# Raw-row routers, a split last tile, scatters that are not held and identity matmuls at the seams of a four-stage kernel

## The reference, cut to what matters

```python
x = L0_attn_a_x                                   # [8, 512, 128] float32
x = x + attn_a(layernorm(x))                      # 16 heads of 8, q and k normalized
x = x + ffn(layernorm(x))                         # routed, 8 experts, top 2, capacity 384
x = x + attn_b(layernorm(x))                      # 16 heads of 64, relative position bias
x = x + ffn(layernorm(x))                         # the same experts again

def ffn(x):                                       # N = 4096 tokens
    logits = xf @ w_router                        # [N, 8]
    probs = softmax(logits); gate, eidx = top_k(probs, 2); gate /= sum(gate)
    pos = cumsum(one_hot(eidx)) - 1               # place of each choice in its expert's list
    keep = pos < C                                # C = 384
    expert_in[e, pos] = xf                        # rows to their slots
    h = relu(expert_in @ w1 + b1); out = h @ w2 + b2
    y = sum(out[e, pos] * gate)                   # back to the tokens, weighted
```

## Time and profile before

| | us |
|---|---|
| median of 3 runs | 1425.36 (1425.13 to 1426.77) |
| profiled execution, its own time | 1422.84 |
| span of its instructions | 1421.1 |
| TensorE busy | 1240.1 (87%) |
| VectorE busy | 933.0 (66%) |
| ScalarE busy | 876.2 (62%) |
| GpSimd busy | 512.1 (36%) |

### The profile page before, as it was taken

The page is one execution under the profiler, slowest core; times in us unless marked ns, Lnnn a source line. Parts: engine busy times, 40 slices in busy tenths (PEclk is TensorE's granted clock), DMA queues, the critical chain, the costliest instruction groups (busy, mean ns, idle before and its releaser), DMA issues.

```text
span 1421.1 us, 22477 instructions
## 1 busy us (share of the span) xinstructions
PE 1240.1 (87%) x6711; PEld 633.6 (45%) x6711; DVE 933.0 (66%) x2823; ACT 876.2 (62%) x1716; POOL 512.1 (36%) x788
## 2 busy tenths in 40 slices
PE   3899999997394899999999999999999999996392
PEld 2333434432272344544544544544544544544272
DVE  5356666664112787798798798798798797794110
ACT  1899898897041776666566576577567566662041
POOL 2000232234373233234334434434433434434255
PEclk7899999999596999999999999999999999999596
DMA  5574344448943465576576577477576565678222
GB/s 156 137 228 143 113 134 138 131 128 232 187 54 53 105 152 149 124 171 159 125 171 163 126 166 168 126 165 159 131 166 150 136 160 142 135 161 225 57 23 23
DMA packets 132937, 197.91 MB, mean 139 GB/s; under 512 B 35167, under 2 KB 76078, under 8 KB 132817
## 3 DMA queue, kind: packets, MB, share of 16 engines
q1 hardware_dynamic: 104848, 138.67, 37.9%
q0 software_dynamic: 27392, 56.76, 19.0%
q10 hardware_dynamic: 576, 1.05, 0.2%
HBM read 61.75 MB, written 39.24 MB: 71 GB/s over the span
## 4 chain that ended last, share of the span: by engine, by line
PE 69%; DVE 10%; issue 7%; DMA 5%; ACT 4%; POOL 3%; SPq 1%; DVEq 0%; POOLq 0%; ACTq 0%
PE s_ps L1461 13%; PE o_ps L922 8%; PE o_psb L1481 8%; PE o_psb L1486 7%; PE score_ps L908 6%; PE m_ps L1452 4%; PE m_ps L1435 4%; PE r_ps L1495 4%; DVE tile L1683 3%; PE r_ps L1452 3%; PE p_ps L1469 3%; DVE blocks L1696 2%; ACT probs_a L629 2%; PE H_f L1105 2%; PE O_f L1118 2%
## 5 line engine op out<-in xcount | busy, mean ns | idle before, releaser
L1597 ACT ACTIVATE tile<-tile,low 128x512 f32<-128x512 f32 x512 | 363.6, 713 | 246.9 <-DVE low L1683 245.6
L1378 POOL DMA_DIRECT2D crossed<-blocks x512 | 253.7, 506 | 488.8 <-DVE blocks L1696 443.7
L1683 DVE CUSTOM_DVE_ANT_0 tile<-s_ps,bias 128x512 f32<-128x512 f32 x512 | 330.2, 681 | 41.7 <-PE s_ps L1461 35.1
L629 ACT ACTIVATE probs_a<-score_ps,gbound 128x1024 f32<-128x1024 f32 x256 | 272.2, 1115 | 51.4 <-PE score_ps L908 51.1
L1461 PE MATMUL s_ps<-kT,qT 64*128 64x512 f32 x1024 | 265.6, 626 | 23.5 <-DVE low L1683 21.8
L1696 DVE STREAM_TRANSPOSE blocks<-tile 128x512 f32<-128x512 f32 x384 | 256.6, 693 | 0.0
L1481 PE MATMUL o_psb<-crossed,v_b 128*64 128x512 f32 x512 | 237.2, 607 | 8.3 <-DMA crossed<-blocks 8.0
L339 POOL DMA_INDIRECT slots<-rows_r,slot_r x128 | 128.5, 1004 | 69.5 <-issue 50.4
L1461 PEld LDWEIGHTS s_ps<-kT,qT 64*128 64x128 f32 x1024 | 85.3, 186 | 138.7 <-issue 80.8
L908 PE MATMUL score_ps<-q_stack,k_stack 32*128 32x512 f32 x512 | 122.8, 501 | 17.8 <-DMA q_stack<-q_parts 13.4
L922 PE MATMUL o_ps<-probs_a,v_ext 128*32 128x512 f32 x1024 | 136.2, 604 | 1.5 <-DVE o_sb L742 1.3
(11 more groups left out here) (157 smaller groups left out, 1619.2 us busy)
## 6 DMA issues: line engine op xcount, KB each, us to landing
crossed<-blocks SPq DMA_DIRECT2D x512, 96.0 KB
crossed<-blocks POOLq DMA_DIRECT2D x512, 96.0 KB
inv_row<-inv_rows SPq DMA_DIRECT2D x128, 128.0 KB, 4.2
q_parts<-parts SPq DMA_DIRECT2D x32, 256.0 KB, 3.8
k_stack<-k_parts SPq DMA_DIRECT2D x32, 256.0 KB, 4.2
q_stack<-q_parts SPq DMA_DIRECT2D x32, 256.0 KB, 4.9
w_f<-in_w SPq DMA_DIRECT2D x32, 256.0 KB, 6.0
k_parts<-parts SPq DMA_DIRECT2D x28, 256.0 KB, 3.5
```

What stands on the lines that cost most here:

```text
L629: nc.scalar.activation(probs[q % 2][:, c % 4 // 2, pair:pair + 2, :].rearrange("p h t -> p (h t)"), score_ps[c % 2][:, :], ACT.Exp, bias=g ...
L1378: pool.dma_start(strip_to(n, a, m), strip_from(n, a, m)).then_inc(crossed_sw[n % 2], 16)
L1597: nc.scalar.activation(tile[(b * NS + k) % RING][s][:, :], tile[(b * NS + k) % RING][s][:, :], ACT.Exp, bias=low[n % 2][:, s, i:i + 1], sc ...
L1683: nc.vector.tensor_tensor_reduce(out=tile[(b * NS + k) % RING][s][:, :], in0=s_ps[k % 2][s][:, :], in1=bias[:, h, off:off + S], scale=1.0, ...
```

## The change

It has five parts.

- **Raw rows in the last batch's router, in both routers.** TensorE turns the raw rows x (`turn_raw`) instead of the normalized ones, and makes logits of them (`logits_raw`). One extra matmul of the all-ones matrix with the router's weights gives the weights' column sums (`column_sums`). VectorE forms mean times column sum (`offsets`), takes it off the raw logits and multiplies by the inverse deviation (`shift_raw`). The copy out of PSUM now stands ahead of `norm_rows`, and `norm_rows` ahead of the use of the logits.
- **The last expert's output by token tiles.** The three tiles go to three PSUM banks, and bias, gate and indirect DMA follow for each tile by itself.
- **Scatters not held.** At the end of `attention_a`, GpSimd no longer waits for the scatters of the last batch but one before it issues those of the last.
- **Identity matmuls.** Ahead of `experts` (both) and of `attention_b`, TensorE makes four matmuls of the identity with a [128, 512] operand, whose results nobody reads (`keep_busy`). In `experts` they wait until GpSimd has issued five of the eight last scatters (`most_sent`); in `attention_b` for the landing of the odd experts' rows in `y_odd`.
- **`values` in `attention_a`** waits for the half of the probabilities that it reads, not for both halves.

```diff
+def keep_busy(nc, g, out, times):
+    for _ in range(times):
+        nc.tensor.matmul(out, g["ident"][:, :], g["ident"][:, :].unsqueeze(1).to_broadcast([P, TB, P]), start=True, stop=True)
...
+    def offsets(self, dve, b, column_sums):
+        wait(dve, self.step, b, self.MOMENTS)
+        dve.wait_ge(self.sums_ps, 1)
+        self.nc.vector.tensor_tensor(self.offset[:, :, :], self.per_tile(self.moments[:, :, 0]),
+                                     self.per_expert(column_sums), ALU.mult).then_inc(self.raw, 1)
+    def copy_raw(self, dve, b, turned):
+        wait(dve, self.turn_ps, b, 1)
+        self.nc.vector.tensor_copy(self.xT[:, :], turned).then_inc(self.raw, 1)
+    def shift_raw(self, dve, b, logits):
+        V = self.nc.vector
+        wait(dve, self.logit_ps, b, 1)
+        dve.wait_ge(self.raw, 1)
+        V.tensor_tensor(self.raw_logits[:, :, :], logits, self.offset[:, :, :], ALU.subtract).then_inc(self.raw, 1)
+        dve.wait_ge(self.raw, 3)
+        V.tensor_tensor(self.offset[:, :, :], self.raw_logits[:, :, :], self.per_tile(self.rstd[:, :]), ALU.mult).then_inc(self.raw, 1)
+        dve.wait_ge(self.raw, 4)
+        V.tensor_reduce(self.top[:, :], self.offset[:, :, :], AX.X, ALU.max).then_inc(self.raw, 1)
+        dve.wait_ge(self.raw, 5)
+        V.tensor_tensor(self.shifted[:, :, :], self.offset[:, :, :], self.per_tile(self.top[:, :]), ALU.subtract).then_inc(self.raw, 1)
...
+    def turn_raw(self, pe, b, turned):
+        for i in range(TB):
+            last = self.nc.tensor.transpose(turned[:, i * P:(i + 1) * P], self.x_tile(b, i), self.g["ident"][:, :])
...
             r.copy_rows(pool, B - 1)
-            r.landed(pool, B - 2)
-            r.scatter(pool, B - 1)
+            r.scatter(pool, B - 1, range(0, 5))
+            pool.sem_inc(most_sent, 1)
+            r.scatter(pool, B - 1, range(5, TOPK * TB))
             r.landed(pool, B - 1)
...
-                if n == 0:
-                    wait(pe, p_ready, b, 4 * q + 4)
-                    if half == 0:
+                wait(pe, p_ready, b, 4 * q + 2 * n + 2)
+                if n == 0 and half == 0:
...
+            before["ready"](pe)
+            keep_busy(nc, g, O_ps[1][:, :], 4)
             turn(0)
             hidden(0)
...
-                        last = nc.tensor.matmul(O_ps[e % 2][:, c * D:(c + 1) * D], hT[e % 2][:, m, c * P:(c + 1) * P],
+                        last = nc.tensor.matmul(out_of(e, c), hT[e % 2][:, m, c * P:(c + 1) * P],
                                                 w2[:, e, m, :], start=(m == 0), stop=(m == HC - 1))
-                last.then_inc(o_ps, 1)
+                    if e + 1 == E_N or c + 1 == CT:
+                        last.then_inc(o_ps, 1)
...
+                    if e + 1 == E_N:
+                        pool.wait_ge(og_ready, e + c + 1)
...
             pe.wait_ge(g["wb"]["loaded"], 16 * (4 + P // COPIES))
+            pe.wait_ge(sent[1], 16 * CT * E_N // 2)
+            keep_busy(nc, g, o_ps[:, :], 4)
```

More of the change, by code:

```diff
@@ L1008, in _ @@
             to_tokens(B - 1, GROUPS - 1)
-            r.turn(pe, B - 1, turned, lambda: None)
-            r.logits(pe, B - 1, logits, lambda: None)
+            wait(pe, r.late, B - 2, r.PLACE)
+            r.column_sums(pe, aux_ps[:, S + 2 * TB * E_N:S + (2 * TB + 1) * E_N])
+            wait(pe, res_done, B - 1, GROUPS)
+            wait(pe, r.step, B - 2, r.SHIFTED)
+            r.turn_raw(pe, B - 1, turned)
+            r.logits_raw(pe, B - 1, logits)
             r.counts(pe, B - 1, counts, lambda: None)
@@ L1139, in _ @@
         def _(dve):
-            for e in range(E_N):
+            for e in range(E_N - 1):
                 dve.wait_ge(o_ps, e + 1)
@@ L1257, in attention_b @@
                      exps=26, first=26, second=28, runs=28, counts=(29, 1), take=29, address=30)
-        R_STEPS = range(20, 31)
         PIECES = [range(2 * n, 2 * n + 2) for n in range(4)]
@@ L1558, in _ @@
                 step(B - 1, d, False, B - 2)
-            for d in R_STEPS:
-                for part in two:
-                    routing(B - 1, d, part)
+            r.column_sums(pe, m_ps[:, 0:E_N])
+            wait(pe, res_done, B - 1, 1)
+            r.turn_raw(pe, B - 1, turned)
+            r.logits_raw(pe, B - 1, logits)
+            r.counts(pe, B - 1, counts, lambda: None)
         @block.scalar
```

73 lines of the change are left out of this document (59 added, 14 removed).

## The result

| us | before | changed |
|---|---|---|
| median (lowest to highest), 4 runs each | 1425.53 (1425.13 to 1426.77) | 1414.48 (1413.8 to 1416.35) |
| profiled execution, its own time | 1422.84 | 1416.35 |
| out of that, its span | 1421.1 | 1414.6 |

The ratio is 0.9931, with a 95% interval of 0.9918 to 0.9945: faster by 11.0 us, where 13.7 were forecast. The time lies in the range (1407.5 to 1417.5), 2.8 us above the forecast of 1411.7. The two profiled executions lie only 6.5 us apart, because the one of before was fast among its runs and the one of the changed kernel slow among its own. I therefore read the two traces seam by seam, from one event to the next. The names in the table: res, VectorE's last addition of the residual; rows, SP's first load of an expert's rows; O, TensorE's first matmul of the first expert's output; s8, the start of the eighth score matmul.

What follows compares the result with a forecast made beforehand. TensorE holds 69% of the chain; the change targets the three seams between stages. Terms 2.1 + 0.5 + 0.6 + 4.1 + 3.3 + 3.1 = 13.7 us give 1411.7 from the 1425.36 median, range 1407.5 to 1417.5.

Steps and rivals of the forecast that it cites:

- Router, third seam: Between `attention_b` and the second expert stage: raw-row routing brings slots, scatters and rows sooner, 3.3 us.
- the rival in which it goes away: GpSimd's 3.21 us stall before the third seam's scatters disappears: 2.7 us more gain, 1409.0 us; chance 0.2.
- Router and hold, first seam: Between `attention_a` and the first expert stage: rows load 2.1 us sooner, limited by the store of x to `x_mid`.
- Identity matmuls, second seam: Between the first expert stage and `attention_b`: turn, projections and first scores run at 2.4 GHz, 4.1 us gained.
- Identity matmuls, third seam: Ahead of the second expert stage: the rows' turn and first hidden layer run at 2.4 GHz, 3.1 us gained.
- Identity matmuls, first seam: Ahead of the first expert stage: TensorE idles 2 to 4 us, the clock mostly falls, 0.5 us gained.
- Last expert by tiles: First expert stage: the last expert's DMAs follow at a shorter gap, 0.6 us; nothing in the second stage.
- the one that lost the clock: Clock falls again between identity matmuls and real work at the second and third seams: 1415.4 to 1418.5 us; chance 0.2.
- The earlier wait of `values`: In `attention_a`: saves some 0.2 us of attention, hidden behind the store of x to `x_mid`.

Runs made afterwards that it cites:

- e11_again: The changed kernel itself, without an edit, timed again on a second chip: median 1419.56 us, ratio 0.9949 to the kernel before.
- e5_bias_four: Changed kernel with four bias parts instead of two loaded behind the first expert's rows: median 1412.43 us, ratio 0.994 to the kernel before.
- e6_hold_back: Changed kernel with GpSimd again waiting for the previous batch's scatters at the end of `attention_a`: median 1417.03 us, ratio 0.9955 to the kernel before.
- e4_five_b: Changed kernel with five identity matmuls instead of four ahead of `attention_b`: median 1415.45 us, ratio 0.9951 to the kernel before.
- e7_more_identity: Changed kernel with twelve identity matmuls ahead of the first expert stage and ten ahead of the second, instead of four: median 1408.85 us, ratio 0.9894.
- e1_no_identity: Changed kernel without any identity matmuls or their waits: median 1418.37 us, ratio 0.997 to the kernel before.
- e9_whole_last: Changed kernel with the last expert's output as one whole again, not by tiles: 1425.59 us in one run, 1426.6 for the kernel before there.
- e3_late_signal: Changed kernel with `most_sent` raised behind the eighth scatter instead of the fifth: median 1414.45 us, ratio 0.994 to the kernel before.
- e12_extra_scatter: Changed kernel with ten/five/ten identity matmuls, four late bias parts and an extra unread indirect DMA behind GpSimd's last row copy: 1413.76 us, ratio 0.9898.
- e10_awake: Changed kernel with ten/five/ten identity matmuls, four late bias parts and a GpSimd memset amid its wait for `attention_b`'s slots: 1413.26 us, ratio 0.9901.

## Why the prediction was right, point by point

The direction and the range held, and so did the terms of the router and of the store of x. The identity matmuls, 7.7 of the 13.7 us, did not: their stretches show 1.94, -0.24 and -1.29, together 0.4. That the time still lies only 2.8 us above the forecast is in good part luck. The seams of the two traces give 6.4 us, less than half of the sum, and the second measurement (`e11_again`) gives 7.0: its ratio, put on the median of before, would be 1418.3, above the range.

- **Router, third seam**: forecast 3.3, measured 3.81 from residual to slots. The term was 0.5 too small. The rows decided, as forecast, but they started 1.16 us after the variance's end (1309.78 after 1308.62) and not 1.48, since GpSimd's power ran sooner, and the four small operations behind them ended within 0.84 us of the rows' end (1310.90 to 1311.74). The stall of 3.2 us moved along, so the rival in which it goes away did not happen.
- **Router and hold, first seam**: forecast 2.1, bounded by the store of x to `x_mid`. From the residual to the rows' load it is 1.42; with the 0.74 by which the residual itself came sooner in this trace, the rows' load moved by 2.16 (378.92 to 376.76). That the load came at the forecast 376.8 leans on these 0.74 us, which no experiment assigns to the change; by its own stretch the term was 0.7 too large. The bound was the right one: `e5_bias_four` takes it away and the rows follow the last scatter again. The store landed 25.4 us after its issue, as forecast (25.1), but the load followed 0.75 us later, not 0.15. `e6_hold_back` shows that without the hold's removal nothing of the router's gain would have come through.
- **Identity matmuls, second seam**: forecast 4.1, measured 1.94. Turn and scores were fast, the projections not. With the clock held all through it is 3.55 (`e4_five_b`), but the kernel without any identity matmuls takes 7.31 us for the same stretch in its trace, where the trace of before has 8.97. By 7.31 the four are worth 0.28 us in the changed kernel, and 1.89 where the clock holds. The term was sized on one execution's clock, and two traces without identity matmuls already differ by 1.7 us.
- **Identity matmuls, third seam**: forecast 3.1, measured -0.24 from slots to O. This is the step that failed, and at the first seam with it. The prediction said that "TensorE is let go when the fifth is issued", 7.5 us before the turn. It is let go when the second starts, since the sequencer runs ahead, and 5.87 us of idling lose the clock. Ten matmuls from the same signal bring 2.8 us (`e7_more_identity`), so the size of 3.1 was right, and its timing wrong.
- **Identity matmuls, first seam**: forecast 0.5, measured -1.29 from rows to O. Nothing ran fast: TensorE idled 8.56 us, not 2 to 4. The hidden layer took 5.42 us, because the clock rose only at its end (386.2 of 380.98 to 386.40); in the earlier trace rows it rose within it (4.40). The identity matmuls are not what cost the 1.29: without any, the stretch takes 10.18 us (`e1_no_identity`), and over the traces without a held clock 8.95 to 10.31. With twelve matmuls the seam gets its 2.9 us.
- **Last expert by tiles**: forecast 0.6, measured 0.36, and the same 0.36 by `e9_whole_last`.
- **Rivals**: the one that lost the clock (0.2) forecast 1415.4 to 1418.5; its mechanism happened at all three seams, and the time, 1414.48, lies just below it: by what TensorE did, this rival and not the main forecast came true. It was forecast for gaps of up to 2 us. The gaps behind it at two seams were of 5.9 and 8.6. On transposes the Trainium skill, "TensorE: Matmul & The Clock Gate", Part 4 (PE-mode transpose), is neither borne out nor refuted: the clock fell right behind a turn made at 2.4 GHz in three traces of the second seam and at three expert seams (turn 0.55 to 0.66 us), and held across it in nine and at five.

Terms as the stages show them: 3.81 + 1.42 + 0.74 + 1.94 + 0.36 - 1.29 - 0.24 - 0.32 (rest) = 6.4 us, the 6.5 us between the two profiled executions. The medians are 11.0 apart. The remaining 4.5 us lie in how those two executions stand in their own runs (2.7 below and 1.9 above the median), and the seams can't tell them. The long stretches between the seams vary by as much: start to res of `attention_a` takes 349.65 to 358.54 us over the fourteen traces, s8 to res of `attention_b` 847.13 to 855.13, and the changed kernel's own two traces differ there by 3.45 and 1.59 us. The earlier wait of `values` was never run alone, so its 0.2 us are neither shown nor refuted. The forecast's "single runs of before differ by 1.6 us" came from three runs; over the other chips they lie between 1420.28 and 1433.85.

## What to carry to other kernels

A semaphore raised by an engine's own queue between DMAs tells when the queue got there, not when the DMAs ran: here it came three to five DMAs early. Work that is meant to keep TensorE's clock has to last until the real work comes, so measure the gap behind it, not only its start, and in more than one execution: ten identity matmuls held it in some traces and lost it in others. Where two conditions stand side by side ahead of a step, as scatters and store at the first seam, shortening one pays only up to the other, and moving two loads behind the step was worth 2.05 us there, where the rewritten router was worth 0.45.

## What the runs showed of the hardware that was not expected

- GpSimd's sequencer was through all eight scatters 3.4 us after the first one started, while the eighth started 9.0 us after it (`e3_late_signal`).
- Ahead of `attention_b` a gap of 1.10 to 1.28 us on TensorE lost the clock in three traces, and one of 1.58 to 1.96 us held it in four; the matmuls ahead of the gap had taken 6.35 to 6.50 us in the first, 5.89 to 6.13 in the second.
- An identity matmul whose operand repeats 128 columns four times costs no more than a plain one: once the clock is up, a matmul of 128x512 in float32 took 0.9 us (20 passes in 10.93 us, the first 4.2 us of it at 1.2 GHz; `e7_more_identity`), against 1.02 to 1.13 for the projections with theirs.
- At the third seam GpSimd's sequencer stalls for 3.2 us ahead of the first indirect DMA behind the last batch's code, in all fourteen traces, whichever DMA that is (`e12_extra_scatter`), with a memset ahead of it (`e10_awake`), and with no DMA packet under way. At the first seam there is none (1.03 us from the slots to the scatter). Why is open.
